# A gated cross-attention block on one core: VectorE's second attention split ahead of a feed-forward finish, and four turns moved into a query product

## The reference, cut to what matters

```python
# attention, 16 heads of 32
Q = layernorm(x) @ W_q.T;  K = ctx @ W_k.T;  V = ctx @ W_v.T
scores = Q K^T / sqrt(32) - slope_h * (query_pos - key_pos)      # masked where mask == 0
e = exp(scores - max);  attn = e / (1 + sum(e))
x = x + tanh(g_xattn) * (attn V) @ W_o.T
# feed-forward
n = layernorm(x);  prev = n shifted by one token
xr = mu_r * n + (1 - mu_r) * prev;  xk = mu_k * n + (1 - mu_k) * prev
x = x + tanh(g_ffn) * sigmoid(xr @ W_r.T) * (relu(xk @ W_k.T) ** 2 @ W_v.T)
```

## Time and profile before

| | |
|---|---|
| median of 3 runs | 1329.17 us (1328.59 to 1329.61) |
| the profiled execution | 1330.07 us |
| its span, first to last instruction | 1328.3 us |
| mean granted TensorE clock | 0.995 of full |
| TensorE busy | 1287.4 us, 97% |
| VectorE busy | 1067.3 us, 80% |
| ScalarE busy | 838.1 us, 63% |
| GpSimd busy | 786.9 us, 59% |

### The profile page before, as it was taken

The page is one execution under the profiler, slowest core; times in us unless marked ns, Lnnn a source line. Parts: engine busy times, 40 slices in busy tenths (PEclk is TensorE's granted clock), DMA queues, the critical chain, the costliest instruction groups (busy, mean ns, idle before and its releaser), DMA issues.

```text
span 1328.3 us, 30833 instructions
## 1 busy us (share of the span) xinstructions
PE 1287.4 (97%) x9848; PEld 1047.3 (79%) x9848; DVE 1067.3 (80%) x2830; ACT 838.1 (63%) x2866; POOL 786.9 (59%) x731
## 2 busy tenths in 40 slices
PE   6999799999999999999999999999999999999998
PEld 6888587878777887777778777778788787878877
DVE  5648688888888888888878888888888888888864
ACT  4327476584839576584948667584948667584932
POOL 0003666666676766666676766667676666667651
PEclk9999899999999999999999999999999999999999
DMA  7763302222030402213040312213040312212000
GB/s 247 249 177 106 95 2 81 79 72 87 32 127 0 126 32 72 86 59 99 17 141 0 105 54 72 86 46 113 8 150 0 88 70 72 86 41 78 10 25 32
DMA packets 75280, 103.72 MB, mean 78 GB/s; under 512 B 26864, under 2 KB 33008, under 8 KB 75248
## 3 DMA queue, kind: packets, MB, share of 16 engines
q1 hardware_dynamic: 75248, 103.31, 25.0%
HBM read 78.62 MB, written 24.67 MB: 78 GB/s over the span
## 4 chain that ended last, share of the span: by engine, by line
PE 79%; DVE 9%; issue 5%; DMA 4%; POOL 1%; ACT 0%; DVEq 0%; POOLq 0%; SPq 0%; ACTq 0%
PE rotating L479 56%; PE score_bank L545 5%; PE attn_bank L649 4%; PE score_bank L479 4%; PE probs_bank L638 4%; PE attn_bank L638 3%; DMA rstd_row<-rstd_scratch 3%; PE score_bank L561 1%; DVE gated L1181 1%; DVE probs L1106 1%; DVE norm L1154 1%; DMA rstd_scratch<-rstd 1%; DVE stats L1142 1%; DVE attn_t L1125 1%; DVE mix_k L1164 1%
## 5 line engine op out<-in xcount | busy, mean ns | idle before, releaser
L856 ACT ACTIVATE probs<-probs,neg_max 128x120 f32<-128x120 f32 x1024 | 390.9, 389 | 6.3 <-DVE neg_max L1110 6.2
L1410 POOL TENSOR_TENSOR probs<-probs,recip 128x960 f32<-128x960 f32 x128 | 232.0, 1813 | 177.7 <-DVE recip L1121 177.7
L1106 DVE SCALAR_TENSOR_TENSOR probs<-mask_in,score_bank 128x120 f32<-128x120 f32 x1024 | 213.8, 271 | 25.2 <-PE score_bank L545 23.8
L479 PE MATMUL rotating<-w_proj,attn_t 128*128 128x512 f32 x768 | 196.7, 406 | 9.9 <-DVE attn_t L1125 9.9
L856 ACT ACTIVATION_READ_ACCUMULATOR probs<-probs,neg_max 128x1 f32 x1024 | 198.4, 194 | 0.0
L479 PE MATMUL rotating<-w_gate,mixed_gate 128*128 128x512 f32 x768 | 194.0, 398 | 0.5 <-POOL mixed_gate L1440 0.5
L479 PE MATMUL rotating<-w_value,xt_or_act 128*128 128x512 f32 x720 | 180.9, 400 | 0.0
L479 PEld LDWEIGHTS rotating<-w_proj,attn_t 128*128 128x128 f32 x768 | 143.5, 192 | 46.8 <-issue 15.7
L479 PE MATMUL rotating<-mixed_key,w_key 128*128 128x512 f32 x720 | 178.8, 397 | 0.0
L479 PE MATMUL rotating<-xt_or_act,w_query 128*128 128x512 f32 x744 | 177.3, 394 | 0.0
L1110 DVE TENSOR_REDUCE neg_max<-probs 128x4 f32<-128x480 f32 x256 | 167.2, 653 | 8.8
(11 more groups left out here) (121 smaller groups left out, 2204.1 us busy)
## 6 DMA issues: line engine op xcount, KB each, us to landing
x_again<-in_x_dram SPq DMA_DIRECT2D x64, 256.0 KB, 2.8
xt_raw<-in_x_t_dram SPq DMA_DIRECT2D x16, 1024.0 KB, 7.8
xs<-in_x_dram SPq DMA_DIRECT2D x64, 256.0 KB, 5.0
out_dram<-gated SPq DMA_DIRECT2D x64, 256.0 KB, 2.0
rstd_row<-rstd_scratch SPq DMA_DIRECT2D x16, 256.0 KB, 5.3
value_scratch<-gated SPq DMA_DIRECT2D x16, 240.0 KB, 2.8
mask_in<-in_mask_dram SPq DMA_DIRECT2D x16, 240.0 KB, 2.8
keys_t<-key_scratch SPq DMA_DIRECT2D x16, 240.0 KB, 4.7
```

The costliest lines, as they stand in the source:

```text
L479: mm = pe.matmul(bank, stationary(a, c), moving(b, c), start=(i == 0), stop=(i == MATMULS - 1))
L856: e = act.activation(probs[:, t % 2, head, :], probs[:, t % 2, head, :], ACT.Exp, bias=neg_max[:, t % 2, head:head + 1], accum_out=sums[:, ...
L1106: z = dve.scalar_tensor_tensor(out=probs[:, t % 2, head, :], in0=neg_dist[:, t, :], scalar=SLOPES[head], in1=score_banks[j][:, g * NK:(g + ...
L1410: pool.tensor_tensor(part, part, recip[:, t % 2, heads].unsqueeze(2).to_broadcast((P, H // 2, NK)), ALU.mult)\
```

## The change

TensorE: `turn2 3` now stands behind the first six matmuls of `query 2` instead of in front of it. The accumulation in the bank of `query 2` goes on behind it. VectorE: `attn_low` of tile 1 now stands in front of `finish` of tile 0 instead of behind it. No instruction is added or removed.

```diff
                 use("query", 0)
                 use("query", 1)
+                use("query", 2, range(6))
                 use("turn2", 3)
-                use("query", 2)
+                use("query", 2, range(6, MATMULS))
                 use("query", 3)
...
                 reciprocals(b, 2, 0)
+                attn_low(b, 1)
                 feed_forward((finish, 0))
-                attn_low(b, 1)
                 bias(b, 3, 2)
```

## The result

The changed kernel takes 1324.18 us (median of 6, 1323.45 to 1325.54), beside 1330.0 for the kernel before in the same sessions (6 runs, 1328.59 to 1331.57). The ratio is 0.995, with a 95% interval of 0.994 to 0.9961: faster by 0.5%. The forecast was 1324.5. The profiled execution took 1324.14 where that of before took 1330.07, 5.93 less; the sum had 5.3. One run of experiment 6 took 2120.1 us at a granted clock of 0.558, where all others had 0.994 to 0.997, and its median is of the other three.

A forecast was written before the change was run, and what follows sets the result against it. TensorE is busy 97% of the span; in the stretch of part A the chain runs through VectorE. The sum was 1330.07 - 4.3 - 1.0 = 1324.8 us, or 1323.9; 1324.5 was taken, range 1320.5 to 1329.0.

The forecast's parts named there:

- the sum: Whole kernel: 1330.07 us of the profiled execution less 4.3 and 1.0, giving 1324.8.
- Part A: Split ahead of first finish: TensorE's 0.65 us stop moves to the first tile's turns; worth 14 x -0.07 = -1.0 us.
- The chain that ended last: In this stretch it bypasses the second projection product, staying on VectorE from the first finish to the first tile's turns.
- the wait of a weight load: TensorE's weight loads already wait for the batch's last bias: 14 times, 4.2 us together, 0.3 each.
- Part A's rest: VectorE behind the moved split, through the last bias: everything moves by only -0.07 us a batch.
- The rival with L1404 holding L1184: GpSimd's one-element instruction blocks VectorE's finish: +0.24 us a batch, 1329.2 or 1328.3 in all, no change; chance 0.14.
- VectorE's wait for ScalarE paid by GpSimd's hold: Ahead of the split VectorE stands some 0.65 us, paid with L1184 falling from 1.46 to near 0.76.
- Rival 4: ScalarE's copy ahead of the split comes later, each 0.1 us costing 1.4; at 0.65 the time is 1333.9; chance 0.06.
- Part B: Fourth tile's turns inside the third query product: seven waits for the normalisation, 0.62 us each, go; gain 4.3 us.
- Part B's cover: Third query product's bank is ready by 0.3 us; moved turns end 7.60 behind query start, before ScalarE's copy at 8.68.
- two readings of the profiled execution: The median is 0.90 us lower than that execution: profiling cost gives 1323.9, fewer waits give 1324.8; 1324.5 was taken.

The follow-up runs named there:

- experiment 6: On the kernel of 5, GpSimd's L1397 and normalisation of tile 3's first half moved ahead of the root of tile 1's variance: 1348.45 us, ratio 1.0146.
- experiment 1: On the kernel before, only the split of attention tile 1 moved ahead of the first finish, turns left in place: 1328.33 us, ratio 0.9995.
- Experiment 3: On the changed kernel, the split of attention tile 1 put between the two instructions of tile 0's finish: 1316.5 us, ratio 0.9908 to the kernel before.
- `turns_only`: On the kernel before, only the fourth tile's turns moved behind the first six matmuls of the third query product: 1324.79 us, ratio 0.9968.
- `norm_first`: On the kernel before, VectorE's normalisation of tile 3 moved ahead of the first query product's read, TensorE's order untouched: 1324.59 us, ratio 0.996.
- experiment 9: On the changed kernel, the fourth tile's turns moved behind the whole third query product: 1324.71 us; behind the fourth: 1350.15 us.
- 4: Two reciprocals of tile 3's first half moved behind the last bias: 1320.63 us on the changed kernel, 1313.77 us on that of Experiment 3.
- 8: On the kernel of 7, the next batch's first statistics of tile 1 moved ahead of VectorE's normalisation of tile 1: 1322.56 us, ratio 0.9953.
- 5: On the changed kernel, the last bias (tile 3, group 3) moved ahead of the residual and statistics of tile 1: 1335.93 us, ratio 1.0053.
- 7: On the kernel of 5, GpSimd's normalisation of tile 3 moved ahead of the root, L1397 made to wait for VectorE's normalisation of tile 1: 1329.26 us, ratio 0.9998.

## Why the prediction was right

- **Part A, the stop is moved, not removed.** Forecast: the turns wait 0.58 longer by the starts. Measured 0.58 (8.16 against 7.58), and experiment 1 shows part A alone at 0.9995, with the wait at its new place. The chain that ended last and the wait of a weight load, and the earlier trace rows, had been the signs.
- **Part A's rest, -0.07 a batch.** A batch without a normalisation wait took 74.79 and takes 74.71 from one second projection product to the next. The term was 0.07 and is 0.08. The rival with L1404 holding L1184 is out: the two overlapped with the small one first, and L1185 took 0.75. Why the small instruction doesn't hold it isn't shown.
- **VectorE's wait for ScalarE paid by GpSimd's hold.** Forecast 0.65, measured 0.69, against 0.71 less on L1185. Experiment 3 shows the hold by another size of it. Rival 4 is out too: ScalarE's copy starts 0.01 behind GpSimd's product as it did before (651.85 and 651.84; 654.55 and 654.54).
- **Part B, 7 x 0.62.** From the first tile's turns in batch 1 to those in batch 14 the kernel takes 971.2 where it took 976.2 and `turns_only` takes 972.0: 5.0 less, 4.2 of it from part B and 0.8 from part A. Both terms are borne out there. Part B alone gave 4.0 of time.
- **Luck in the total.** From the second projection product of batch 0 to that of batch 15 it is 1125.2 against 1130.45, 5.3 less, but 0.3 of that lies in batch 0, where the sum had nothing and where the same stretch differs by 1 us between these kernels. Another 0.6 of the span lies outside, 0.9 less in the tail and 0.25 more at the start; in the tail TensorE's wait for GpSimd's mixed keys is 0.4 and was 1.9 by the view of waits. That wait is 0.3 in `turns_only` and 1.9 in `norm_first`, which take the same time, and what sets it was not followed up. None of this is a term of the sum, and the 0.3 by which the forecast lay under the sum was a choice between two readings of the profiled execution.
- **Part B's cover.** The bank of the third query product was ready, ScalarE's copy was not later (8.66 behind the query start, 8.68 before), and experiment 9 shows where that ends.
- **What was judged less well.** The gain of part B depends on how many batches wait, and I took the trace's 7. In the changed kernel the normalisation ends behind the turns' old place (6.0 against 5.6 behind the query start) in 11 of the 14, in `turns_only` in 5, and in experiment 1 nine waited: the 7 was one draw of a number that a tenth of a microsecond decides. The kernel before spread over 1327.2 to 1331.7 in one session of 16 runs, and `turns_only` over 1324.1 to 1325.2 in 6; that the number of waits makes this spread was not shown run by run.
- **Wrong in the experiments** were my sizes where the next meeting point was GpSimd (4, 8), the sign in 5, where I had put the price on the wrong engine's queue, and 6 and 7, where the moved GpSimd instruction held another of VectorE's.

## What to carry to other kernels

When a busy engine waits for a queue that is itself never idle, look for the next place at which the two meet: moving one item up the queue moves the stop there, and only what shortens the queue, or moves work behind its last meeting point, is kept. A wait can be hidden on either side of it, by doing other work first on the waiting engine or by taking the awaited work out from behind a slow load. Before putting an instruction forward, ask which standing time of its engine it used to fill, and before moving a GpSimd instruction, which of VectorE's will then run beside it.

## What the runs showed of the hardware

- Large GpSimd instructions with two inputs hold VectorE's two-input and tensor-scalar instructions on SBUF to their own end: L1184 ended 0.55 behind L1410, and L1190 0.55 behind L1420 although it started 1.22 behind its start instead of 0.88. The tensor-scalar L1154 ended 0.28 behind L1440, whether it ran 0.86 or 1.67 us.
- I had not expected that so small a one as L1120 (128x8) is held too: 0.84, 0.98 and 1.25 us in place of 0.16, each over 0.02 to 0.03 behind an L1397.
- GpSimd's one-element L1404/L1405, started 0.04 to 0.06 ahead of a two-input VectorE instruction in 14 batches, did not hold it (0.75 us).
- Whether an instruction is held turns on about a tenth of a microsecond between the two starts: L1154 took 0.55 when it started 0.18 ahead of L1440, which then took 1.51, and 1.38 when it started 0.19 behind, with L1440 at 1.29. It was held as well when it started 0.06 and 0.10 ahead.
